# Where a graph layer's one-hot matrices are made, and how far ahead its edge terms and node steps run

## The reference: what is computed

```
h = relu(layernorm(x)) @ enc_w + enc_b              # [12500, 128]
for l in range(3):
    e   = edge_attr @ edge_w[l] + edge_b[l]          # [212500, 16] @ [16, 128]
    msg = relu(h[src] + e)
    agg = segment_sum(msg, dst)
    z   = (1 + eps[l]) * h + agg
    h   = relu(relu(z @ mlp_w1[l] + mlp_b1[l]) @ mlp_w2[l] + mlp_b2[l])
    keep h
out = x + concat(h0, h1, h2, h3) @ out_w + out_b
```

## Time and profile before

| what | value |
|---|---|
| median of 3 runs | 7435.4 us |
| the profiled execution's own time | 7395.73 us |
| its span | 7393.9 us |
| mean granted TensorE clock | 0.558 of 2.4 GHz |
| busy: POOL, PE, DVE, ACT | 64%, 65%, 23%, 14% |

### The profile page before, as it was taken

The page is one execution under the profiler, slowest core; times in us unless marked ns, Lnnn a source line. Parts: engine busy times, 40 slices in busy tenths (PEclk is TensorE's granted clock), DMA queues, the critical chain, the costliest instruction groups (busy, mean ns, idle before and its releaser), DMA issues.

```text
span 7393.9 us, 56283 instructions
## 1 busy us (share of the span) xinstructions
PE 4774.5 (65%) x14396; PEld 3131.3 (42%) x14397; DVE 1663.8 (23%) x4168; ACT 999.7 (14%) x1597; POOL 4751.3 (64%) x5075
## 2 busy tenths in 40 slices
PE   5666666666666646666666666673666666666667
PEld 4444444444444424444444444442444444444444
DVE  4222222222222212222222222221222222222222
ACT  4111111111111101111111111110111111111111
POOL 5666666666666466666666666646666666666664
PEclk7555555555555555555555555555555555555555
DMA  3122212222222112222222222211111111111112
GB/s 116 53 54 54 55 53 54 54 55 54 54 54 54 44 49 54 55 55 54 54 55 55 53 54 56 55 43 51 51 51 52 51 52 51 52 51 51 52 52 72
DMA packets 191126, 404.82 MB, mean 55 GB/s; under 512 B 85159, under 2 KB 87927, under 8 KB 190439
## 3 DMA queue, kind: packets, MB, share of 16 engines
q0 software_dynamic: 159456, 326.88, 17.0%
q1 hardware_dynamic: 21759, 56.75, 2.6%
q10 hardware_dynamic: 9840, 20.48, 0.8%
HBM read 378.08 MB, written 25.69 MB: 55 GB/s over the span
## 4 chain that ended last, share of the span: by engine, by line
another core or an unknown queue 44%; PE 27%; issue 18%; DVE 6%; DVEq 3%; ACT 3%; POOL 0%; DMA 0%; ACTq 0%
PE bank L624 14%; PE bank L620 9%; DVE rows L879 3%; ACT rows L543 2%; DVE onehot L865 2%; PE bank L651 1%; PE bank L664 1%; PE bank L643 1%; DVEq L939 1%; DVE agg_t L875 1%; PE bank L645 1%; DVEq L247 1%; DVEq L875 0%; PE bank L661 0%
## 5 line engine op out<-in xcount | busy, mean ns | idle before, releaser
L372 POOL DMA_INDIRECT rows<-h_table,idx x4983 | 4714.0, 946 | 2575.5 <-issue 1417.7
L624 PEld LDWEIGHTS bank<-onehot,rows 128*128 128x128 f32 x9966 | 2178.6, 310 | 3367.3 <-ACT rows L543 1966.2
L624 PE MATMUL bank<-onehot,rows 128*128 128x64 f32 x9966 | 2158.1, 394 | 2162.8 <-ACT rows L543 1599.7
L620 PE MATMUL bank<-edgew,attr 65*128 65x512 f32 x2496 | 2279.0, 1026 | 9.6 <-DMA w2s<-w 9.6
L543 ACT ACTIVATE rows<-rows 128x512 f32<-128x512 f32 x1248 | 783.1, 628 | 5381.1 <-DVE rows L879 4213.0
L875 DVE TENSOR_TENSOR agg_t<-bank,agg_t 128x64 f32 x1248 | 278.1, 223 | 4790.4 <-remote 3542.9
L879 DVE TENSOR_TENSOR rows<-bank,rows 128x512 f32<-128x512 f32 x1248 | 857.6, 687 | 83.2 <-DMA rows<-h_table,idx 35.2
L620 PEld LDWEIGHTS bank<-edgew,attr 65*128 65x128 f32 x2496 | 677.7, 316 | 280.6 <-issue 280.6
L865 DVE TENSOR_TENSOR onehot<-bank,dst_rel 128x256 f32<-128x256 f32 x1248 | 518.3, 415 | 205.4 <-issue 205.4
L651 PE MATMUL bank<-hid,w2s 128*128 128x512 f32 x300 | 195.3, 769 | 192.5 <-ACT hid L506 124.8
L664 PE MATMUL bank<-outw,h_t 128*128 128x128 f32 x588 | 151.7, 423 | 62.0 <-ACT h_t L515 58.5
(11 more groups left out here) (83 smaller groups left out, 478.6 us busy)
## 6 DMA issues: line engine op xcount, KB each, us to landing
rows<-h_table,idx POOLq DMA_INDIRECT x4983
attr<-ea_t SPq DMA_DIRECT2D x156, 256.0 KB
h_table<-h_n ACTq DMA_DIRECT2D x48, 256.0 KB
h_table<-rows SPq DMA_DIRECT2D x24, 256.0 KB, 2.1
out<-out_acc SPq DMA_DIRECT2D x24, 256.0 KB
out_acc<-x_t ACTq DMA_DIRECT2D x4, 1280.0 KB, 11.5
rows<-dst_g SPq DMA_DIRECT2D x1, 832.0 KB
rows<-dst_t SPq DMA_DIRECT2D x1, 832.0 KB
```

Source lines behind the costliest of these rows:

```text
L372: return g.indirect_dma_start(dst, None, h_table[l % 2], bass.IndirectOffsetOnAxis(ap=index, axis=0))
L620: return nc.tensor.matmul(dst[0:EP, 0:tiles * D], cols, edgew[:, l, 0:tiles * D], start=True, stop=True)
L624: last = nc.tensor.matmul(dst[:, 0:WIN], rows[0:EP, slot, j, :], onehot[0:EP, hot_slot, j, :], start=(j == 0), stop=(j == tiles - 1))
```

## The change

- DVE's `one_hot` leaves the edge loop. ACT makes the one-hot in two steps: `targets_apart` (four activations of 128x64, Abs of `dst_rel - iota`, the target as a per-partition bias) three groups ahead, and `one_hot` (one activation of 128x256, Relu of `1 - that`, with a tile of ones as bias) two groups ahead. Both stand behind the relu of each group. A new semaphore `apart_made` orders the two steps. The ring of one-hot matrices has eight slots where it had four.
- The PSUM bank that held `iota_ps` becomes a fourth bank of `e_ps`. PE issues edge terms three groups ahead, and over the ends of rounds: groups 13, 14 and 15 of a round issue the terms of groups 0, 1 and 2 of the next.
- DVE's two delayed `accumulate` steps also run over the ends of rounds: its loop starts at group 2 of a round and ends at group 1 of the next.
- The steps of a node unit are spread: PE after groups 1, 3 and 5 of the half (1, 2, 3 before), ACT behind 2, 4 and 7 (2, 3, 5), DVE behind 6 (4), where it also looks up the unit's number.
- The pass for windows wider than 64 nodes keeps DVE's one-hot; it isn't entered with these edges.

```diff
-NE_PS = 3
+NE_PS = 4
 NA_PS = 2
-NHOT = 4
+AHEAD = 3
+NHOT = 8
...
-        e_ps = bank[0:NE_PS]
-        agg_ps = bank[NE_PS:NE_PS + NA_PS]
-        iota_ps = bank[5][:, 0:WIN]
+        e_ps = [bank[i] for i in (0, 1, 2, 5)]
+        agg_ps = bank[3:3 + NA_PS]
...
+            g.memset(ones[:, :], 1.0).then_inc(s_const, 1)
...
+                def targets_apart(b, k):
+                    hot = onehot[0:EP, k % NHOT, 0:real_tiles(b, k), :]
+                    for j in range(real_tiles(b, k)):
+                        last = nc.scalar.activation(hot[:, j, :], iota[0:EP, :], ACT.Abs, scale=-1.0,
+                                                    bias=dst_rel[0:EP, bass.ds((b * RING + k) * TG + j, 1)])
+                    last.then_inc(apart_made, 1)
+
+                def one_hot(b, k):
+                    hot = onehot[0:EP, k % NHOT, 0:real_tiles(b, k), :]
+                    act.wait_ge(apart_made, b * RING + (l * NG + k + 1 + S0))
+                    nc.scalar.activation(hot, hot, ACT.Relu, scale=-1.0, bias=ones[0:EP, 0:1])
+
+                def ahead(step, b, k, n, groups):
+                    if k + n < groups:
+                        step(b, k + n)
+                    elif not isinstance(b, int):
+                        step(b + 1, k + n - RING)
...
                         nc.scalar.activation(part, part, ACT.Relu).then_inc(relued, 1)
-                        if kk in (2, 3, 5)[:3 if l < L - 1 else 2] and groups - half * HB >= HB:
+                        ahead(targets_apart, b, k, 3, groups)
+                        ahead(one_hot, b, k, 2, groups)
+                        if kk in (2, 4, 7)[:3 if l < L - 1 else 2] and groups - half * HB >= HB:
...
+                for k in range(3):
+                    targets_apart(0, k)
+                for k in range(2):
+                    one_hot(0, k)
...
-                    for k in range(min(2, groups)):
-                        e_terms(k)
-                    for k in range(groups):
+                    for k in range(RING):
...
-                        if k + 2 < groups:
-                            e_terms(k + 2)
+                        if k + AHEAD < RING:
+                            e_terms(b, k + AHEAD)
+                        elif not isinstance(b, int):
+                            e_terms(b + 1, k + AHEAD - RING)
                         sums(k)
-                        if kk in (1, 2, 3) and groups - half * HB >= HB:
+                        if kk in (1, 3, 5):
...
+                for k in range(AHEAD):
+                    e_terms(0, k)
...
-            own(v.tensor_copy(iota_ps, iota[:, :]))
...
+                def edge_group(b, k, before):
+                    half, kk = k // HB, k % HB
+                    if kk == 0:
+                        dve.load(bases[half * HB:(half + 1) * HB], base_row[0:1, bass.ds(b * RING + half * HB, HB)])
+                    if before:
+                        accumulate(*before)
+                    dve.wait_ge(e_done, b * RING + (l * NG + k + 1 + S0))
+                    dve.wait_ge(gathered[k], (b + (l * uses_of_slot(k) + 1)) * (16 * TG))
+                    add_terms(k, e_ps[k % NE_PS], real_tiles(b, k)).then_inc(summed, 1)
+                    if kk == 6:
+                        unit = load_unit(dve, b * 2 + half)
+                        with dve.If(unit > 0):
+                            node_take(unit_before(unit))
...
+                for k in range(NA_PS):
+                    edge_group(0, k, None)
                 with nc.Fori(0, NFULL, engines=(mybir.EngineType.DVE,), hint_back_edge=True) as b:
-                    edge_body(b, RING)
-                edge_body(NFULL, REST)
+                    for k in range(NA_PS, RING):
+                        edge_group(b, k, (b, k - NA_PS))
+                    for k in range(NA_PS):
+                        edge_group(b + 1, k, (b, k + RING - NA_PS))
```

More of the change, by code:

```diff
@@ L110, in gnn_kernel @@
         lneps = sb("lneps", [P, 1])
+        ones = sb("ones", [P, 1])
         first_root = sb("first_root", [P, 1])
@@ L195, in gnn_kernel @@
         summed = sem("summed")
+        apart_made = sem("apart_made")
         relued = sem("relued")
@@ L207, in gnn_kernel @@
         N_PAR = 7
-        N_CONST = 10
+        N_CONST = 11
         block = ctx.enter_context(nc.Block())
@@ L407, in _ @@
         def _(act):
+            act.sem_inc(apart_made, S0)
             for s in (hid_ready, h_ready):
@@ L543, in edge_body @@
                         nc.scalar.activation(part, part, ACT.Relu).then_inc(relued, 1)
-                        if kk in (2, 3, 5)[:3 if l < L - 1 else 2] and groups - half * HB >= HB:
+                        ahead(targets_apart, b, k, 3, groups)
+                        ahead(one_hot, b, k, 2, groups)
+                        if kk in (2, 4, 7)[:3 if l < L - 1 else 2] and groups - half * HB >= HB:
                             with act.If(unit > 0):
-                                (relu_z if kk == 2 else relu_h if kk == 3 else store)(unit_before(unit))
+                                (relu_z if kk == 2 else relu_h if kk == 4 else store)(unit_before(unit))
+                for k in range(3):
+                    targets_apart(0, k)
+                for k in range(2):
+                    one_hot(0, k)
                 with nc.Fori(0, NFULL, engines=(mybir.EngineType.Activation,), hint_back_edge=True) as b:
@@ L673, in _, with e_terms, edge_body @@
                 pe.wait_ge(s_w, l * 32 + 32)
-                def edge_body(b, groups):
-                    first_group = b * RING + l * NG
[L678 to L683, removed]
+                def e_terms(b, k):
+                    half, kk = k // HB, k % HB
+                    if kk == 0:
+                        wait_apart(pe, attr_in[half], (b + (l * uses_of_half(half) + 1)) * 16)
+                    edge_terms(e_ps[k % NE_PS], attr[half][:, kk * EP:(kk + 1) * EP], l, real_tiles(b, k))\
+                        .then_inc(e_done, 1)
+                def edge_body(b):
+                    first_group = b * RING + l * NG
                     def sums(k):
@@ L923, in node_take @@
                      .then_inc(o_added, 1)
[L925 to L951, removed]
@@ L953, in _, with accumulate @@
-                with nc.Fori(0, NFULL, engines=(mybir.EngineType.DVE,), hint_back_edge=True) as b:
-                    edge_body(b, RING)
-                edge_body(NFULL, REST)
+                def accumulate(b, k):
+                    group = b * RING + l * NG
+                    base = dve.snap(bases[k], min_val=0, max_val=NP)
+                    dve.wait_ge(agg_done, group + (k + 1 + S0))
+                    dve.wait_ge(added, group + (k + S0))
+                    add_window(base, agg_ps[k % NA_PS]).then_inc(added, 1)
@@ new lines, in _ @@
+                for k in range(NA_PS):
+                    edge_group(0, k, None)
+                with nc.Fori(0, NFULL, engines=(mybir.EngineType.DVE,), hint_back_edge=True) as b:
+                    for k in range(NA_PS, RING):
+                        edge_group(b, k, (b, k - NA_PS))
+                    for k in range(NA_PS):
+                        edge_group(b + 1, k, (b, k + RING - NA_PS))
+                for k in range(NA_PS, RING):
+                    edge_group(NFULL, k, (NFULL, k - NA_PS))
@@ L956, in _ @@
+                for k in range(RING - NA_PS, RING):
+                    accumulate(NFULL, k)
                 first = load_left(dve)
```

6 lines of the change are left out of this document (4 added, 2 removed).

## The result

The changed kernel takes 7460.16 us, median of 7 runs (7454.38 to 7464.09), against 7437.33 us for the kernel before (7 runs, 7432.07 to 7442.63). The ratio is 1.0031, 95% interval 1.0019 to 1.0042: slower by 0.3%, where I had forecast 0.6% faster. The profiled execution took 7460.16 us.

A forecast was written before the change was run, and what follows sets the result against it. POOL's gathers and its pauses on the full ring were taken as the bound. Terms 0 + 0 + 2 - 45 + 0 = -43 us took the profiled 7395.7 to 7353; with 39.7 to the median, 7392 us, range 7300 to 7500.

The forecast's parts named there:

- The bound: POOL's gathers at 1.25 us each take 6229 of 7394 us; pauses on the full ring take 871 us.
- The law of the pauses: POOL on the full ring: a pause costs about 2.2 us however short the burst, some 0.55 us a group more beyond 3.
- ACT makes it ... so 0.: One-hot on ACT: 1.87 us a group, 2.50 with its relu, below PE's 3.41 and POOL's 5.0, so costs 0.
- The first groups' one-hots: One-hots on ACT ahead of each layer's first relu: 5.1 us, of which 2 us was taken to show in layer 0.
- DVE's one-hot: 0: Taking the one-hot off DVE, 0.416 us a group or 518 us in all, is hidden by its wait for `agg_done`: 0.
- No drain between rounds: At round boundaries, queued adds and sums continue, so a burst of one group joins its neighbour: -45 us over 78 rounds.
- Three ahead: Edge terms on PE three groups ahead: DVE never waits for the terms, so the third group is worth 0 within a round.
- node steps: Node unit steps spread in the edge loops: could win 26 us or cost 43 us, taken as 0.
- The slower one: Rival: ACT's turn exceeds 3.41 us a group, bursts fall to 3 groups, 107 us, 7540; with other losses, chance 0.26.
- milder 7490: The slower rival's half-size case, where bursts shorten only in some places: 7490 us; no separate chance given.
- The pauses vanish: Rival: PE's results are late through program order that the change removes, so 871 us go: 6564 us, chance 0.05.

The follow-up runs named there:

- `after_dve_hot4`: The changed kernel with the one-hot back on DVE, iota read from SBUF: 7383.2 us against 7401.7 for the kernel before in the same job, ratio 0.9975.
- `act_hot4`: The kernel before with only the one-hot moved to ACT: 7416.2 us against 7401.7 for the kernel before in the same job, ratio 1.0020.
- `two_ahead`: The changed kernel with edge terms two groups ahead, not three: 7420.7 us against 7401.7 for the kernel before in the same job, ratio 1.0026.
- `units`: The kernel before with only the node steps spread: 6321.2 us, ratio 0.9998 to the kernel before in the same job.
- `old_units`: The changed kernel with the node steps where they were before: 7409.5 us against 7401.7 for the kernel before in the same job, ratio 1.0011.
- `half_gathers`: The kernel before, but behind the first ring POOL gathers only two of each group's four tiles: 4094.8 us against 6333.9, one run.
- `more_incs`: The kernel before, with SP incrementing an unwaited semaphore 512 times behind each load of attr, 64 a group: 11020.1 us, 49% more.

## Why the prediction was wrong, point by point

**The bound.** Right: POOL's 1.25 us a gather and its pauses on the full ring. The law of the pauses held roughly. By the prediction's own way of taking 5.0 us a group out of the distance, a pause is 3.0 us after the bursts of four above, where the law gives 2.75, and 3.5 us after the two of five in `after_dve_hot4`, where it gives 3.3.

**"ACT makes it ... so 0."** This step failed, and decides the sign. The single durations were about right, 0.333 and 0.493 us. Their sum was not what ACT needs: four Abs take 1.05 us together, and ACT's whole turn with its relu is 1.87 us (from the relu at 1868.62 to the next at 1870.49) where I had 2.50. So ACT's busy share rose to 35% and not 45%, and there was more room than I counted. The Trainium skill, "ScalarE: Activation LUTs" (What ACT_TABLE_LOAD costs), gives the same two durations, and it also lets back-to-back activations overlap by about 93 ns, which the prediction's estimate of 1.83 us by that page leaves out; the trace agrees with both. Even so the step wasn't free: I had priced it only by the time on its own engine. In a held job five more activations and what goes with them, 8,800 instructions on the page (56283 to 65092), go with PE's results coming late earlier. On the old order the step costs 14.5 us (`act_hot4`). On the new order it costs 37.5 us in one job (`two_ahead` against `after_dve_hot4`, which differ also in one group of lead of the edge terms and in where `iota` is read), and between the result (+0.31%) and `after_dve_hot4` (-0.25%), two jobs, it is 0.56% or some 41 us. How much of it is the bare instructions and how much the relu behind them stays open.

**The first groups' one-hots: 2.** Nothing against it: POOL's longest wait, the one at the start, is 31.3 us against 30.7.

**DVE's one-hot: 0.** No run takes it away without giving it to ACT, so this term isn't shown by itself. With it kept and ACT's added, the loss was 50.7 us.

**No drain between rounds: -45.** The sign was right, the size too large. Order, banks and node steps together gave -18.5 us with `iota` read from SBUF, which costs 7 us (0.1%) in a free job; if it costs the same here, about -25. The drain itself went: behind more than 9 us of idle time PE dispatches a round's first sums in 28 of 75 rounds in before and in none in the changed kernel. But this isn't what gains, for `act_hot4`, which keeps the drain, has 4 of 75. And the burst of one group was no burst of every round, as I had read it off one stretch: only 15 of before's start at the round's last group, as that one does. The bursts of one that I wanted gone are 76 in `after_dve_hot4` and 90 in the changed kernel, against 56 before. They don't belong to the round's end alone, and the price of 78 boundaries rested on that.

**Three ahead: 0, node steps: 0.** `two_ahead` (1.0026) can't be told from the change (1.0031), in another job. `units` is 0.9998 in a free job. `old_units` at 1.0011 lies 0.2% below the change: a hint that spreading costs 15 us in a held job, from one run in another job, so left open.

**The rivals.** The slower one has bursts getting shorter, and they did, to four groups and not to three; 7460 us lies below its milder 7490. Its condition, a turn of ACT above 3.41 us, didn't come: the turn is 1.87 us. Relus did come late at times, and whether that costs is open, as said. "The pauses vanish" came true in a way that I hadn't thought of: not by the change, but in every free job, for both kernels, at 6321 to 6334 us. It also takes more than the 871 us that I priced: before takes at least 1068 us less there than in any held job of the experiments. The rule of the Trainium skill, "SBUF — State Buffer" (Who interferes with whom), that PE never waits on anyone agrees with the free jobs and not with the held ones.

**What stays open** is what makes a job held. One difference stands beside it. The traces of held runs lack most of the semaphore updates: 24121 are recorded for the kernel before, 92506 for `units` in a free job, which updates as often. Nearly all that lack are updates by DMAs, 18107 against 84239. And "remote" in the waits, an event without its instruction, is 903 us of POOL's waiting in one and absent in the other. That would fit a hold that comes from the recording of events, instructions and increments, and that everything executed adds to. More landings, which are recorded too, cost nothing that can be told, which speaks against the simplest form of it. No run here shows a kernel without the recording, so this is argued and not shown. Another difference isn't separated either: in my held jobs each kernel was executed once, in the free ones ten times (`half_gathers` once); the result, with 7 executions, was held, so it isn't their number alone.

## What to carry to other kernels

An instruction that is hidden in its own engine's idle time can still cost: here some 9,000 more instructions beside a stream of indirect gathers cost 0.2 to 0.5% where results came late, and nothing where they didn't. The durations of instructions on one engine don't add up to its turn: read the turn from the timeline, from one start to the next. When a wait in a trace ends long after the work it waits for (15 us here, with all counts arriving together), don't price the program's order as if that lateness belonged to it; first run the unchanged kernel in another job and see whether the lateness is the kernel's. And compare only within a job: the same program differed by 17% between two of them, on one chip.

## What the runs showed of the hardware

In a held job one semaphore increment on SyncE follows the other after 66 ns in the mean away from gathers and after 299 ns in the mean beside them (59 ns in the median both times), at 1.25 us a gather (`more_incs`). TensorE's counts arrive up to 15 us late there, and most of POOL's pauses in the stretches shown end 2 to 4 us after it stops. The same kernels in a free job have no wait of POOL for the ring above 0.3 us. Activations of 128x64 and 128x256 with a pointer bias from SBUF last 0.333 and 0.493 us, and four of the first take 1.05 us together. Reading one operand of a DVE comparison from SBUF in the place of PSUM cost 0.1% of the kernel; why was not looked into.
